# Cross-attention and mixture-of-experts layer on one core: attention probabilities made transposed, with fp32 weighting and rounds of five slots

## What is computed

```python
# cross-attention, 16 heads of 16
qh, kh, vh = proj(layernorm(x)), proj(ctx), proj(ctx)       # y = x @ w.T + b
attn = softmax(qh @ kh.T / sqrt(16))                          # 77 keys
x = x + (attn @ vh) @ w_o.T + b_o
# 8 experts of width 1024, two for each token
h = layernorm(x)
probs = softmax(h @ router_w); top_w, top_i = top_k(probs, 2)
for e in range(8):
    out += cw[:, e] * ((silu(h @ gate_w[e]) * (h @ up_w[e])) @ down_w[e])
x = x + out
```

## Time and profile before

| what | value |
|---|---|
| median of three executions | 978.47 us |
| the profiled execution's own time | 979.63 us |
| its span, first to last instruction | 977.9 us |
| mean granted TensorE clock | 0.964 |
| TensorE matmul busy | 861.9 us (88%) |
| VectorE busy | 640.6 us (66%) |
| ScalarE busy | 474.2 us (48%) |
| GpSimd busy | 269.5 us (28%) |

### The profile page before, as it was taken

How to read it: one execution, slowest core, us unless ns; L and a number is a source line. 1 busy time by engine, 2 the same in 40 slices (tenths; PEclk the granted TensorE clock), 3 DMA queues, 4 the chain that set the end, 5 groups by cost and what they waited for, 6 DMA issues and landing times.

```text
span 977.9 us, 32075 instructions
## 1 busy us (share of the span) xinstructions
PE 861.9 (88%) x12176; PEld 780.1 (80%) x12176; DVE 640.6 (66%) x1938; ACT 474.2 (48%) x903; POOL 269.5 (28%) x315
## 2 busy tenths in 40 slices
PE   1789988898888860699999999999999999999996
PEld 0567777677676640689999999999999999999995
DVE  4688989988989765367547446645744746544443
ACT  2578877777777743344325334323533534332221
POOL 2112544434544346012212112121111212211111
PEclk9999999999999865799999999999999999999999
DMA  7112222222322113352522522522342252222221
GB/s 222 29 41 56 76 89 67 62 75 63 99 66 61 49 62 130 123 166 52 161 55 34 157 33 54 157 33 56 72 123 56 44 173 34 33 33 34 33 33 17
DMA packets 69214, 73.70 MB, mean 75 GB/s; under 512 B 19739, under 2 KB 62952, under 8 KB 69160
## 3 DMA queue, kind: packets, MB, share of 16 engines
q1 hardware_dynamic: 45128, 33.11, 11.8%
q0 software_dynamic: 12944, 17.87, 10.6%
q10 hardware_dynamic: 11088, 22.02, 6.5%
HBM read 45.31 MB, written 26.39 MB: 73 GB/s over the span
## 4 chain that ended last, share of the span: by engine, by line
PE 51%; DVE 5%; DMA 5%; ACT 3%; issue 2%; ACTq 1%; POOL 1%; POOLq 0%; DVEq 0%; SPq 0%
PE bank L463 11%; PE bank L465 11%; PE bank L464 11%; PE bank L651 5%; PE bank L653 5%; PE bank L652 5%; DMA raw<-expert_rows 4%; PE bank L626 2%; DVE e_lo L1063 1%; DVE h_full L1182 1%; ACT h_hi L792 1%; DMA expert_rows<-rows,slot_u 1%; ACT g_act L790 1%; DVE h_lo L1188 1%; ACTq L306 1%
## 5 line engine op out<-in xcount | busy, mean ns | idle before, releaser
L463 PE MATMUL bank<-xg,e_hi 128*128 128x128 f16 x2176 | 372.7, 219 | 0.7 <-DVE xg L1159 0.6
L464 PE MATMUL bank<-xg,e_hi 128*128 128x128 f16 x2176 | 372.7, 219 | 0.0
L465 PE MATMUL bank<-xg,e_lo 128*128 128x128 f16 x2176 | 372.6, 219 | 0.0
L1334 POOL DMA_INDIRECT out<-y_sb,tok_row x68 | 113.5, 1669 | 470.3 <-DVE y_sb L1177 446.8
L463 PEld LDWEIGHTS bank<-xg,e_hi 128*128 128x128 f16 x2176 | 213.4, 98 | 2.0 <-issue 0.8
L464 PEld LDWEIGHTS bank<-xg,e_hi 128*128 128x128 f16 x2176 | 213.4, 98 | 0.8
L465 PEld LDWEIGHTS bank<-xg,e_lo 128*128 128x128 f16 x2176 | 213.4, 98 | 0.0
L790 ACT ACTIVATE g_act<-bank 128x512 f32<-128x512 f32 x136 | 81.3, 598 | 248.6 <-PE bank L465 233.3
L1182 DVE SCALAR_TENSOR_TENSOR h_full<-bank,g_act 128x512 f32<-128x512 f32 x136 | 94.0, 692 | 129.5 <-ACT g_act L790 121.8
L651 PE MATMUL bank<-e_hi,h_hi 128*128 128x256 f16 x544 | 148.4, 273 | 3.7 <-DVE h_lo L1188 3.7
L652 PE MATMUL bank<-e_lo,h_hi 128*128 128x256 f16 x544 | 148.3, 273 | 0.0
(11 more groups left out here) (166 smaller groups left out, 1754.5 us busy)
## 6 DMA issues: line engine op xcount, KB each, us to landing
raw<-expert_rows SPq DMA_DIRECT2D x68, 132.5 KB, 2.5
e_stage<-in_gate_w ACTq DMA_DIRECT2D x7, 1024.0 KB
e_stage<-in_up_w ACTq DMA_DIRECT2D x7, 1024.0 KB
e_stage<-in_down_w ACTq DMA_DIRECT2D x7, 1024.0 KB
expert_rows<-pads SPq DMA_DIRECT2D x8, 530.0 KB, 3.5
xin<-in_x SPq DMA_DIRECT2D x16, 256.0 KB, 2.8
xres<-in_x SPq DMA_DIRECT2D x16, 256.0 KB, 2.9
out<-x SPq DMA_DIRECT2D x16, 256.0 KB
```

The costliest lines, as they stand in the source:

```text
L463: pe.matmul(dst, a_hi(c), b_hi(c), start=c == 0, stop=False)
L464: pe.matmul(dst, a_hi(c), b_lo(c), start=False, stop=False)
L465: mm = pe.matmul(dst, a_lo(c), b_hi(c), start=False, stop=c == chunks - 1)
L1334: pool.indirect_dma_start(out, bass.IndirectOffsetOnAxis(tok_row[:], 0), y_sb[:], None, compute_op=ALU.add).then_inc(added, 16)
```

## The change

Attention of a batch is reordered. Scores are made twice. The first time they are made with the high parts alone, in six units (6, 6 and 4 heads for each half of the queries), and only for the row maxima. All maxima of a batch are turned on TensorE (`turn_max`) and copied (`max_t`). The second time, in the next round, they are made transposed: `score_t` makes [128 head-and-key rows, 256 queries] for the two halves of the heads in one bank, five groups of up to 128 rows (16 heads x 77 keys are two halves of 616 rows), and a fourth matmul takes the maximum off in PSUM (`own_max`). The exponential reads PSUM and writes fp32 probabilities that already stand turned. `weigh_values` takes them as fp32 stationary operand against fp32 values `v_own`, zero outside the own head, 34 or 51 columns for each matmul. `v_own` is made by VectorE from a projection with wide, repeated context (`cx_hi`, `cx_lo` three times as wide, in two buffers). The biases of the values and of the output become one row, added in `project_o` by a matmul. The round has five slots, one for each group, and its order is written out anew on each engine. All 12 weight pieces of expert 0 are split in rounds 3 to 5, and the load of expert 1 is issued before the last five rounds.

```diff
-HG = 4
-UNITS = NT * H // HG
+GROUPS = 5
+REPEATS = 3
+HEAD_UNITS = ((0, 6), (6, 12), (12, 16))
+UNITS = NT * len(HEAD_UNITS)
-EARLY = 8
+EARLY_FROM, EARLY_TO = 3, 6
...
+            def load_next():
+                act.wait_ge(e_lo_ready, PIECES)
+                load_expert(act, 1)
+            batches(act, body, load_next)
...
-            def round_of(j):
-                load_a(j)
-                spread_keys(j - 1)
-                store_c(j - 3)
-                load_c(j - 2)
+            def round_of(n, loads=True):
+                spread_keys(n - 1)
+                if loads:
+                    load_cx(n + 1)
+                store_c(n - 3)
+                load_c(n - 2)
+                if loads:
+                    load_x(n + 1)
...
+            def score_t(j, g):
+                par = j.plus % 2
+                bank = ps_scores_t[(j.plus * GROUPS + g) % 2]
+                if g == 0:
+                    after(pe, max_t_ready, j.value(1, 1))
+                    after(pe, q_lo_ready, j.value(KC, KC))
+                after(pe, exp_ready, j.value(GROUPS, g - 1))
+                rows = slice(g * P, g * P + rows_of(g))
+                for m in range(KC):
+                    keys = [k_diag[:, par, l, m, :, :].rearrange("p h k -> p (h k)")[:, rows] for l in range(2)]
+                    dst = bank[0:rows_of(g), m * S:(m + 1) * S]
+                    pe.matmul(dst, keys[0], q_hi[:, par, m, :], start=True, stop=False)
+                    pe.matmul(dst, keys[0], q_lo[:, par, m, :], start=False, stop=False)
+                    pe.matmul(dst, keys[1], q_hi[:, par, m, :], start=False, stop=False)
+                    mm = pe.matmul(dst, own_max[:, m, :, :].rearrange("h a k -> h (a k)")[:, rows], max_t[:], start=False, stop=True)
+                mm.then_inc(st_made, 1)
+            def weigh_values(j, g):
...
+                for m in range(KC):
+                    for t in range(NT):
+                        mm = pe.matmul(ps_att[t][:, (m * HEADS + first) * VW:(m * HEADS + end) * VW],
+                                       probs_t[0:rows, g, m * S + t * P:m * S + (t + 1) * P],
+                                       v_own[0:rows, par, m, head_at(g):head_at(g + 1), :].rearrange("k h w -> k (h w)"),
+                                       start=g == 0 and m == 0, stop=g == GROUPS - 1, skip_group_check=True)
...
+                    mm = pe.matmul(ps_c[:, t * D:(t + 1) * D], row_ones[:], bo_parts[:], start=False, stop=True)
...
+            def own_values(j):
+                after(dve, v_made, j.value(1, 1))
+                after(dve, pv_made, j.value(GROUPS, -GROUPS))
+                for g in range(GROUPS):
...
+                    dve.tensor_tensor(v_own[0:rows, j.plus % 2, :, head_at(g):head_at(g + 1), 0:DK],
+                                      ps_a[0:rows, cols].rearrange("k (m h w) -> k m h w", m=KC, w=DK),
+                                      own_head[0:rows, g, first:end].unsqueeze(1).unsqueeze(3).broadcast_to([rows, KC, end - first, DK]),
+                                      ALU.mult).then_inc(v_ready, 1)
+            def exponentials(j, g):
+                after(act, st_made, j.value(GROUPS, g + 1))
+                after(act, pv_made, j.value(GROUPS, g + 1 - GROUPS))
+                rows = rows_of(g)
+                act.activation(probs_t[0:rows, g, :], ps_scores_t[(j.plus * GROUPS + g) % 2][0:rows, :], ACT.Exp,
+                               scale=S_SCALE).then_inc(exp_ready, 1)
```

More of the change, by code:

```diff
@@ L53, with rows_of, heads_of, head_at @@
 SPREAD = HEADS * 16
+def rows_of(g):
+    return min(P, HEADS * KS - g * P)
+def heads_of(g):
+    return g * P // KS, (g * P + rows_of(g) - 1) // KS + 1
+def head_at(g):
+    return sum(end - first for first, end in map(heads_of, range(g)))
+SHARES = head_at(GROUPS)
 class At:
@@ L495, in project_q, with score @@
                 mm.then_inc(q_made, 1)
-            def score(i, par, u):
-                t, v = divmod(u, UNITS // NT)
-                m, half = divmod(v, 2)
+            def score(j, u):
+                par = j.plus % 2
+                t, (first, end) = unit_heads(u)
                 if u == 0:
-                    after(pe, q_lo_ready, i.value(KC, KC))
-                    after(pe, kd_ready, i.value(SPREAD, SPREAD))
-                after(pe, shifted, i.value(UNITS, u - 1))
-                keys = [k_diag[:, par, l, m, half * HG:(half + 1) * HG, :].rearrange("p h k -> p (h k)") for l in range(2)]
-                three(ps_score[u % 2][:, 0:HG * KS],
-                      lambda c: q_hi[:, par, m, t * P:(t + 1) * P], lambda c: q_lo[:, par, m, t * P:(t + 1) * P],
-                      lambda c: keys[0], lambda c: keys[1], 1).then_inc(s_made, 1)
@@ L596, in body @@
             def body(n, a, b, c, r, z):
[L597 to L615 removed]
+                if a:
+                    turn_x(a)
@@ new lines, in body @@
+                if r:
+                    router(r)
+                if c:
+                    project_o(c)
+                if a:
+                    score(a, 1)
+                if b:
+                    weigh_values(b, 1)
+                if b:
+                    score_t(b, 3)
+                if a:
+                    score(a, 2)
+                    project_v(a)
+                if r:
+                    ranks(r)
+                if a:
+                    score(a, 3)
+                if b:
+                    weigh_values(b, 2)
@@ L617, in _ @@
+                if a:
+                    score(a, 4)
+                if b:
+                    score_t(b, 4)
+                if a:
+                    score(a, 5)
+                if b:
+                    weigh_values(b, 3)
+                if n:
+                    project_k(n)
+                if a:
+                    turn_max(a)
             batches(pe, body)
@@ L1077, in between, with run @@
                         next(chain, None)
[L1079 to L1081 removed]
+                def run(stage, *args):
+                    stage(*args)
+                    between()
                 def start(chain):
                     under_way.append(chain)
[L1086 to L1093 removed]
@@ L1129, in body @@
+                if c:
+                    run(low_att, c)
+                if a:
+                    run(maximum, a, 0)
                 while under_way:
                     under_way = [chain for chain in under_way if next(chain, False) is None]
+                if r:
+                    start(route_top(r))
+                    between()
+                if a:
+                    run(maximum, a, 1)
+                    run(maximum, a, 2)
+                if c:
+                    run(residual, c)
+                    run(sum_x, c, 1, x2, x2_ready, 1, x2_summed)
@@ new lines, in body @@
+                if a:
+                    run(maximum, a, 3)
+                if m:
+                    start(statistics(m, n, c))
+                if a:
+                    run(own_values, a)
+                    run(maximum, a, 4)
+                    run(maximum, a, 5)
+                    run(shrink_max, a)
+                if n:
+                    run(full_k, n)
+                if a:
+                    run(copy_max, a)
+                while under_way:
+                    under_way = [chain for chain in under_way if next(chain, False) is None]
```

494 lines of the change are left out of this document (253 added, 241 removed).

## The result

The changed kernel takes 1094.45 us (median of 4 runs, 1091.48 to 1096.36) where the kernel before takes 978.4 (4 runs): a ratio of 1.118, 95% interval 1.115 to 1.121. It is slower, and by far more than the forecast 1028; the time lies outside the range as well. The profiled executions differ by 115.1 us (spans 1093.0 and 977.9), and that difference is what I divide up here.

The account below looks back on a forecast made before the run. It took VectorE as nearly full in the filled rounds, TensorE close behind. Start +3, rounds +42, drain -12 and clock +18 gave +51 us on the 978.47 median: 1029, stated as 1028 us, range 965 to 1090.

Parts of the forecast that it names:

- idle edge: Start of each round: TensorE has nothing it may start before the turn of x, 4.2 us.
- The clock: TensorE's granted clock in the batch rounds: falls in two rounds of three, 1.8 us each, +18 us.
- The narrow matmuls: TensorE's added work in a round: score_t 4.35 us, two bias rows 0.2, with no extra for few rows.
- W: The new fp32 weighting on TensorE, 20 matmuls a round: 5 us at 0.25 each, ends 2.4 and 9.8.
- rival A: fp32 weighting at four full loads, W = 9.8: round 26.3 us, total 1090; chance 0.15.
- The round: Filled batch round walked in the new order: 16.7 + 1.2 + 4.2 = 22.0 us against 20.15.
- The early rounds: First three batch rounds, with fewer stages but the same edge and single score bank: 18.6, 20.3 and 21.5 us.
- The +4 for weight pieces: Rounds 3 to 5 carry four weight pieces each, delaying ScalarE and VectorE: about 4 us each.
- The start: Before the first batch: VectorE's small copies and bias parts come before k_diag's clearing, +3 us.
- The drain: From the last batch to the experts: e_lo gone, scatter and row load freed by loading expert 1 earlier, -12 us.
- Rival C: The edge does not open and TensorE's work alone sets rounds of 17 us: total 951, or some 930; chance 0.19.
- Rival B: Cheap weighting, W = 2.4, and no clock loss, edge stays: round 20.9 us, total 990 to 1000; chance 0.13.

Follow-up runs that it names:

- e1_warm: Changed kernel plus 60 unused fp16 matmuls of 128 columns on TensorE at each filled round's end; filled rounds 22.95 us in place of 27.3, clock 1.00.
- e4: Changed kernel with the turn of x moved behind the last weighting and two score_t; 1056.6 us, 1.037 times the kernel before on its chip.
- e2: Changed kernel with the 16- and 33-row operands filled with zeros to 128 rows; four of five rounds 24.7 to 24.9 us, under 27.3.
- e3: Changed kernel with values and probabilities in fp16, low parts left out; filled rounds 23.9 us in place of 27.3, clock 0.75.
- e7: Order of e6 on the changed kernel, plus operands filled to 128 rows; 991.4 us, 1.011 times the kernel before.
- e9: e8 with VectorE clearing k_diag and max_t as its first work; 976.1 us, ratio 0.994 to the kernel before.
- c2: Kernel before the change with only k_diag's clearing moved to be VectorE's first work; 976.6 us, ratio 0.994.
- e6: Changed kernel in a second order: turns of x and of the rows later, their inputs reordered; 1019.7 us, 1.041 times the kernel before.
- e8: e7 with expert 0's weight pieces spread three to a round over four earlier rounds; 982.3 us, ratio 1.0007 to the kernel before.

## Why the prediction was wrong

The direction was right, and so was the mechanism, an idle edge in each round. The size was not. By its own steps:

- **The clock, the step that failed.** "I take a fall in two rounds of three, each costing some 1.8 us (3.6 at half, ...)": +18 in all, 1.2 a round. Measured, it falls in every round from 70 us on and stays at half for some 10 us, 4.3 us of a filled round by e1_warm and 50 over the 15 distances (400.8 less the 351.1 of e1). The prediction names no row for the 3.6 us at half clock; the only fall that it shows is that of the earlier trace rows, where TensorE had paused for under 1 us. The other rows of before that bear on it, the windows at the start of its expert stage, have the clock back 2.5 us after the work begins:

```profile
399.00:401.50 2.50, 2.45 (x24) 2.48 (x25) 0.00 (x0) 0.00 (x0) 0.00 (x0) 0.50 0.21 54
401.50:404.00 2.50, 2.50 (x46) 2.50 (x45) 0.00 (x0) 0.78 (x1) 0.00 (x0) 0.96 0.02 7
```

  I read no row of before with 10 us of full work at half clock. Behind the new edge, with TensorE 91 to 100% busy, it took four times as long as at the start of the experts. The Trainium skill ("TensorE: Matmul & The Clock Gate", "HAM oscillation") says that gaps between bursts bring the clock down each time. On that the trace of the changed kernel agrees with it and not with my two in three; behind e4's shorter gaps it was three in four.
- **The narrow matmuls, a term that I left out.** I priced `score_t` at 0.11 a matmul and the two bias rows at 0.2 together, whatever their height. The 12 with 16 or 33 rows cost 2.4 us more a round; e2 took 29.5 us off the 15 distances.
- **W** was 4.15 against my 5, within the ends of 2.4 and 9.8; rival A, a W of 9.8, is refuted although its total, 1090, is nearly the time measured.
- **The round.** I had 22.0 + 1.2 of clock = 23.2. With the measured clock (+3.1), narrow operands (+2.4) and W (-0.85) it is 27.9, and 27.3 was measured: the walk itself was right within 0.6. Its edge was 3.7 us idle where I had 4.2, the steps 0.2 each, the norm 1.09, all as walked. VectorE's 14.5 a round was 15.1 (56.3 of 102), ScalarE 8.0.
- **The early rounds** were 20.8, 26.5 and 27.4 against 18.6, 20.3 and 21.5. The third is shorter in e1 (24.1) and in e2 (25.6), so it has the same two reasons; the second falls to 22.6 in e2. The first does not: e1, e2 and e3 leave it at 20.8, and what its walk missed stays open. The +4 for weight pieces in three rounds did not show (27.3 like the rest); once the edge was gone it did, as 4 to 6 us a round in e7.
- **The start** was +3.2 against +3. The added constants make 1.7 of it (the clearing of `k_diag` starts at 15.2 us where it was 13.5); the rest comes behind it, in the small steps of the first layer norm, which take 5.0 us where they took 3.6. So the sum was near in part by luck. The clearing itself is in both kernels, and e9 and c2 show that both wait for it.
- **The drain** was +4.7 against -12. What I took out of it did go: the scatters issue at 0.97 us each and the row load lands 2.2 us after its issue. Its clock is 0.64, but before had 0.66 there, so a low clock is nothing that the change brought. The narrow operands are: with their height alone changed it takes 75.7 us at 0.73 (e2) in place of 85.5, and 71.1 at 0.77 (e7) in place of 88.5 at 0.53 (e6), near the 69 of the forecast. So most of the miss goes with the term that I left out; how much of it is the matmuls' own time and how much a clock that came back sooner is not separated.
- **Rival C** (the edge is covered, 930 to 951) named the right condition, that the order decides, but the order has to be changed for it. Its rounds of 17 are not reached even then: e7 and e8 take 19.45, just above the 19.3 from which C counts, and e8's whole is indeed that of before. TensorE is busy 17.1 us in such a round (89.6 of 102), so rounds of 17 would leave it no idle time at all. **Rival B** (cheap weighting, no loss of clock) fails by its second condition.

The sum by terms: start +3.2; distances +106.2, of which the clock 50 (e1), the narrow operands 30 (e2), and 26 what is left, the idle edge less what TensorE was relieved of; drain +4.7; experts +1.0; together 115. e1 and e2 were each made alone, so that the 50 and the 30 add up is assumed. What holds the clock down for 10 us behind the edge, when 2.5 us were enough at the start of the experts and over 40 were not in e6's drain, stays open. It is not the fp32 weighting (e3 has it as well, at a clock of 0.75); the rest of the difference in the work (fp32 turns, matmuls of many small forms) no run separates.

## What to carry to other kernels

Idle time of the engine that sets the pace costs more than its length: look at the granted clock behind each gap until it is back (it took from 2.5 to over 40 us here), and cost a gap that comes back each round with it. When an engine is relieved, ask for each round what is the last input to come and what stands in front of it in each queue; the relief was real here (VectorE from 92 to 56 of 102 us) and worth nothing until the order was rewritten. And before a gain of a repaired version is put down to its idea, give the old kernel the same side edits.

## What the runs showed of the hardware

- A matmul whose operands have 16 or 33 rows breaks the train of weight loads: 0.20 us to it and 0.21 from it, where neighbours of 128 rows stand 0.11 apart. Filling up to 128 rows with zeros removes it (e2).
- A true fp32 matmul with 34 or 51 columns takes 0.21 to 0.22 us and leaves two records, at 0.105 each.
- After 3.7 us idle, TensorE's clock was at the lower level for 10 us of nearly full work (0.50 in four windows); it fell as well after pauses of 2.23 us (e4, both times) and of 1.6 us (once of two), and in e6's drain it stayed there for 42.5 us of full work.
